# A transformer block on one core: in the attention loop the transposed scores go ahead of the scores for the maximum, an output half is copied out right behind its group, and the projection stage's normalization and loads are reordered

## The reference

```python
def _L0_attn_ref(x, Wq, bq, Wk, bk, Wv, bv, Wo, bo):
    Q, K, V = proj(Wq, bq), proj(Wk, bk), proj(Wv, bv)
    Q = Q * cos + _rotate_half(Q) * sin
    K = K * cos + _rotate_half(K) * sin
    scores = jnp.einsum('bhqd,bhkd->bhqk', Q, K) / scale
    scores = jnp.where(causal, scores, jnp.float32(-jnp.inf))
    attn = jax.nn.softmax(scores, axis=-1)
    out = jnp.einsum('bhqk,bhkd->bhqd', attn, V)
    return out.transpose(0, 2, 1, 3).reshape(B, S, H) @ Wo.T + bo
def _L0_ffn_ref(...):
    hdn = silu((xf @ gate_w.T) * gate_s) * ((xf @ up_w.T) * up_s)
    return (hdn @ down_w.T) * down_s
x = x + _L0_attn_ref(_layernorm(x), ...)
x = x + _L0_ffn_ref(_layernorm(x), ...)
```

## Time and profile before

| | |
|---|---|
| runs | 768.98, 772.01, 768.7 us |
| profiled execution | 772.27 us, its span 770.6 us |
| PE busy | 740.3 us (96%), 3563 instructions |
| PEld busy | 540.8 us (70%) |
| DVE busy | 437.1 us (57%) |
| ACT busy | 303.1 us (39%) |
| POOL busy | 245.6 us (32%) |
| chain that ended last | PE 75%, DVE 6%, ACT 5%, issue 5%, DMA 5% |
| TensorE's granted clock | 0.997 of full speed on the mean |

### The profile page before, as it was taken

One profiled execution on the slowest core, in us unless ns is written; L12 is line 12 of the kernel. 1 busy time (PEld: TensorE's weight loads), 2 busy tenths in 40 slices (PEclk: granted clock), 3 DMA queues, 4 the chain that ended last, 5 costly groups with the idle time before them and its releaser, 6 DMA issues.

```text
span 770.6 us, 10665 instructions
## 1 busy us (share of the span) xinstructions
PE 740.3 (96%) x3563; PEld 540.8 (70%) x3563; DVE 437.1 (57%) x1103; ACT 303.1 (39%) x641; POOL 245.6 (32%) x224
## 2 busy tenths in 40 slices
PE   7998999989999999999999989999999999999996
PEld 7786888765555555555555546787788888888885
DVE  7868493987777767777777726783325114315112
ACT  3231222255555555555555563223332223223221
POOL 0724161502114141414141416832223223223223
PEclk9999999999999999999999999999999999999999
DMA  8584659645656666666566554680001001001001
GB/s 279 210 280 166 219 202 298 257 134 153 155 157 184 157 174 157 166 155 182 157 181 157 141 158 136 223 353 0 1 1 55 0 1 54 0 0 56 0 1 57
DMA packets 54318, 104.39 MB, mean 135 GB/s; under 512 B 14820, under 2 KB 18404, under 8 KB 53748
## 3 DMA queue, kind: packets, MB, share of 16 engines
q1 hardware_dynamic: 54264, 103.72, 44.0%
HBM read 69.62 MB, written 38.21 MB: 140 GB/s over the span
## 4 chain that ended last, share of the span: by engine, by line
PE 75%; DVE 6%; ACT 5%; issue 5%; DMA 5%; POOL 2%; SPq 1%; DVEq 0%; POOLq 0%; ACTq 0%
PE ps L1096 31%; PE ps L1235 17%; PE ps L1311 9%; PE ps L1121 8%; PE ps L1214 8%; ACT p L679 4%; DMA x_st<-in_x 2%; PE ps L1088 1%; ACT o_raw L686 1%; DMA q_st<-neg_max_T 1%; POOL hid_lo L592 1%; DMA w_st<-in_wk 1%; DVE stats L770 1%; DVE xn L785 1%; DMA rec_l<-rec_rows 1%
## 5 line engine op out<-in xcount | busy, mean ns | idle before, releaser
L679 ACT ACTIVATE p<-ps 128x384 f32<-128x384 f32 (+3 forms) x384 | 162.5, 487 | 127.3 <-PE ps L1214 126.8
L842 DVE CUSTOM_DVE_ANT_0 masked<-ps,mask_qk 128x512 bf16<-128x512 f32 (+1 forms) x240 | 114.3, 502 | 77.3 <-PE ps L1121 76.2
L1235 PE MATMUL ps<-p,v_slot 128*64 128x512 f32 (+3 forms) x768 | 137.3, 493 | 7.7 <-ACT o_raw L686 7.6
L1214 PE MATMUL ps<-q_st,k_st 99*128 99x384 f32 (+2 forms) x384 | 134.8, 369 | 2.0 <-DMA q_st<-neg_max_T 1.1
L1121 PE MATMUL ps<-k_st,q_st 96*128 96x512 f32 (+2 forms) x384 | 130.8, 362 | 1.5 <-DVE row_max L842 1.3
L1047 DVE SCALAR_TENSOR_TENSOR hid<-ps,us_sb,silu 128x512 f32<-128x512 f32 x44 | 33.0, 750 | 165.2 <-PE ps L1096 159.5
L592 POOL TENSOR_TENSOR hid_lo<-hid,hid_hi 128x512 fp32r<-128x512 f32 x44 | 56.8, 1290 | 173.0 <-ACT hid_hi L757 173.0
L1235 PEld LDWEIGHTS ps<-p,v_slot 128*64 128x64 f32 x768 | 53.0, 136 | 80.8 <-issue 55.6
L561 POOL TENSOR_SCALAR_AFFINE_SELECT p<-p 128x512 f32<-128x512 f32 x64 | 41.0, 641 | 214.3 <-ACT p L679 214.3
L1121 PEld LDWEIGHTS ps<-k_st,q_st 96*128 96x128 f32 x384 | 72.2, 189 | 31.3 <-issue 21.8
L1214 PEld LDWEIGHTS ps<-q_st,k_st 99*128 99x128 f32 x384 | 72.2, 189 | 20.7 <-ACT p L679 8.8
(11 more groups left out here) (119 smaller groups left out, 1075.1 us busy)
## 6 DMA issues: line engine op xcount, KB each, us to landing
qk_scratch<-st_hi SPq DMA_DIRECT2D x32, 512.0 KB, 3.8
q_st<-qk_scratch SPq DMA_DIRECT2D x32, 384.0 KB, 4.1
k_st<-qk_scratch SPq DMA_DIRECT2D x32, 384.0 KB, 5.2
flag_st<-in_ffn SPq DMA_DIRECT2D x32, 264.0 KB, 2.8
ffn_copy<-in_ffn SPq DMA_DIRECT2D x32, 264.0 KB, 3.3
qk_scratch<-st_lo SPq DMA_DIRECT2D x16, 512.0 KB, 3.7
o_T<-o_raw SPq DMA_DIRECT2D x32, 128.0 KB, 4.1
rec_l<-rec_rows SPq DMA_DIRECT2D x32, 128.0 KB, 3.4
```

What stands on the lines that cost most here:

```text
L679: act.activation(p32[:, at:at + q0 + w - keep], ps[:, ST_BANK + i % ST_RING, keep - q0:w], ACT.Exp, scale=SCALE).then_inc(exp_done, 1)
L842: ins = dve.tensor_tensor_reduce((masked_a if u < 2 else masked)[:, s_before(i) % 2, col:col + kept], scores, mask_qk[:, 512 - kept:512], ...
L1214: pe.matmul(ps[:, ST_BANK + i % ST_RING, 0:w], k_st[0:K_ALL, slot, kt * P:(kt + 1) * P], q_st[0:K_ALL, slot, q0:q0 + w], start=True, stop= ...
L1235: ins = pe.matmul(ps[VW * a:VW * (a + 1), o_bank(u, half), q0 - 512 * half:512], v_slot[:, slot, kt, :], p32[:, at:at + n], start=(kt == 0 ...
```

## The change

Four orders change; no instruction is added or removed.

1. TensorE, stage B: at each position `shifted_piece(t, i)` is issued before `transpose_max(t + 1)` or `score_bank(t + 2, i)`, not behind it.
2. ScalarE, stage B: `evacuate_half(u, 0)` comes behind exponential 3 instead of exponential 6 of an even step.
3. VectorE and ScalarE, stage A: in chunks 1 and 2 the next chunk's statistics come before `rotate(0)` and its normalization directly behind it (before: behind `rotate(0)` and behind `low(0)`), and `std_of` ahead of `high(0)`. In chunk 0 the statistics come ahead of `weight_lo(3)`, and `std_of(1)` ahead of `weight_hi(5)`.
4. SyncE, stage A: the load of chunk `c + 2` of x is issued in chunk `c` ahead of the stores of `p` = 3, not at the start of chunk `c + 1`. For chunk 2 this takes it past those stores and past `load_late` (Wo's load).

```diff
@@ sync
             for c in range(N_CH):
                 b, cc = divmod(c, CC)
-                if 2 <= c + 1 < N_CH:
-                    sp.wait_ge(ln_done, c + 2)
-                    load_x(x_st[:, :, :], c + 1).then_inc(x_in, 16)
...
                 for p in range(4):
+                    if p == 3 and c + 2 < N_CH:
+                        sp.wait_ge(ln_done, c + 3)
+                        load_x(x_st[:, :, :], c + 2).then_inc(x_in, 16)
@@ scalar
                 if c == 0:
                     weight_hi(4)
+                elif c < N_CH - 1:
+                    std_of(c + 1)
                 high(0)
                 if c == 0:
+                    std_of(1)
                     weight_hi(5)
-                if c < N_CH - 1:
-                    std_of(c + 1)
                 high(1)
...
-                    if t % 2 == 0 and t >= 2 and i == PV_AFTER[0][0] + 3:
+                    if t % 2 == 0 and t >= 2 and i == PV_AFTER[0][0]:
                         evacuate_half((t - 2) // 2, 0)
@@ vector
+                def next_statistics():
+                    dve.wait_ge(x_in, 16 * (c + 1))
+                    ln_first(c + 1, x_tiles)
+                def next_tokens():
+                    dve.wait_ge(t_ps, TJ * (c + 1))
+                    ln_second(c + 1)
+                if 0 < c < N_CH - 1:
+                    next_statistics()
                 rotate(0)
                 if c == 0:
+                    next_statistics()
                     weight_lo(3)
-                if c == N_CH - 1:
+                elif c < N_CH - 1:
+                    next_tokens()
+                else:
                     dve.wait_ge(row_max_init, 1)
                     dve.wait_ge(ln_done, N_CH + 1)
-                if c < N_CH - 1:
-                    dve.wait_ge(x_in, 16 * (c + 1))
-                    ln_first(c + 1, x_tiles)
                 rotate(1)
                 low(0)
-                if 0 < c < N_CH - 1:
-                    dve.wait_ge(t_ps, TJ * (c + 1))
-                    ln_second(c + 1)
...
@@ tensor
                 for i in range(NPC):
+                    if t < HEADS:
+                        shifted_piece(t, i)
                     if i == M_ENTRY and t < HEADS - 1:
                         transpose_max(t + 1)
                     elif i != M_ENTRY and t + 2 < HEADS:
                         score_bank(t + 2, i)
-                    if t < HEADS:
-                        shifted_piece(t, i)
```

More of the change, by code:

```diff
@@ L925, in _ @@
                 if c == 0:
-                    dve.wait_ge(t_ps, TJ)
-                    ln_second(1)
+                    next_tokens()
                 if c == N_CH - 1:
```

## The result

| | before | changed |
|---|---|---|
| runs, us | 768.98, 772.01, 768.7, 771.51, 770.85 | 766.8, 763.55, 764.84, 762.3, 765.38 |
| median | 770.85 | 764.84 |
| profiled execution (span) | 772.27 (770.6) | 766.8 (765.1) |
| ratio | | 0.9924, 95% interval 0.99 to 0.9947 |

The change makes the kernel 6.0 us or 0.76% faster.

What follows compares the result with a forecast made beforehand. TensorE, busy 740.3 of 770.6 us, was taken as the bound, so only its waits or slow clock could be won. Terms 1.8 + 4.4 + 0.8 + 0.3 = 7.3 us gave 763.4 us, range 759 to 768.5.

Steps and rivals of the forecast that it cites:

- one of its signs: Projections, chunk 0: TensorE's p = 3 would run without a gap, where it stood idle 1.57 us before.
- Chunk 1, forecast 4.4 us: Projections, chunk 1: earlier x removes the stalls for rotate(1) and rotate(2) and the lower clock; 4.4 us, bounds 2 and 4.5.
- The second rival: Projections: x comes too late and, with statistics ahead of rotate(0), delays everything; 4.4 falls to 1 or 2, 766 us; chance 0.13.
- Chunk 0, forecast 1.8 us: Projections, chunk 0: statistics fill VectorE's 2.00 us wait, so TensorE's stall at p = 3 goes; 1.8 us, bounds 0 and 2.0.
- weight_lo(3) 1.7 more: Chunk 0, VectorE: after the statistics end at 22.8, weight_lo(3) takes 1.7 us and ends at 24.5, ahead of rotate(1).
- Attention, forecast 0.05 us in a pair: Attention, pair of steps: -0.12 ahead of group 0, +0.07 odd step, 0 even step; 0.8 us in 15 pairs.
- The 0.3 us from steps 0 and 1: Attention's first two steps: pieces run ahead of TensorE's wait for VectorE's maxima; 0.3 us gained.
- Attention gives it back: Rival: projections gain, but score banks behind waiting pieces cost 5.4 us against 6.2, leaving about 768 us; chance 0.17.
- Attention gains more: Rival: ScalarE's earlier start carries through, 13 us at most in 15 pairs; half gives about 757 us; chance 0.10.
- The slower case: Rival: each step's first piece waits for the maximum's rows, 0.5 us in each of 31 steps; 778 us; chance 0.05.
- The sum itself, 7.3 us: Whole kernel: 1.8 for chunk 0, 4.4 for chunk 1, 0.8 for attention pairs and 0.3 for steps 0 and 1.
- the middle between 765.0 and 761.7: Forecast median 763.4 us, between 7.3 off the profiled 772.27 and 7.3 off the median 768.98.

Runs made afterwards that it cites:

- e4: Kernel before with only the load of x for chunks 2 and 3 issued ahead of the stores of p = 3; ratio 0.9955.
- e5: Kernel before with only VectorE's and ScalarE's new order in the projections, x loaded at the old place; ratio 1.0107, slower.
- e6: Changed kernel, but at positions 5 to 9 the shifted piece again goes behind the score bank; ratio 0.9913 to the kernel before.
- e10: e7 with the DRAM-to-DRAM copy of feed-forward weights issued behind the next head's loads; ratio 0.9882 to the kernel before.
- e1: Kernel before with only the projection changes: VectorE's and ScalarE's new order and the early load of x; ratio 0.9948.
- e7: e6 with the copy of half 1 moved to directly behind its group, behind exponential 9 of the odd step; ratio 0.9858 to the kernel before.
- e8: Changed kernel with the copy of half 1 moved behind exponential 9 of the odd step; ratio 0.9916 to the kernel before.
- e2: Kernel before with only TensorE's attention order changed, shifted piece ahead of the score bank at each position; ratio 0.9993.
- e9: Kernel before with the early load of x and both output halves copied early, old orders elsewhere; ratio 0.9871.
- e11: e9 with the DRAM-to-DRAM copy of feed-forward weights issued behind the next head's loads; ratio 0.9862 to the kernel before.
- e12: e9 with VectorE's test of the feed-forward weights moved from behind position 3 to behind position 9; ratio 0.9986 to the kernel before.

## Why the prediction was right

The forecast was 763.4 us with a range of 759 to 768.5; the median is 764.84. The largest term was right in cause and size. One term was mis-sized, and one of its signs failed: chunk 0's p = 3 still has a gap of 0.88 us in the profile.

**Chunk 1, forecast 4.4 us: right.** It gave 4.49, the clock included. The late load was named as the cause, and e4 shows that it alone gives the whole term. What the prediction did not say is that part 3 gives nothing in this chunk; by e5 it needs the early load and costs 4.4 us without it. The second rival had this danger right and its size too small. It was near: rotate(1) ended 0.3 us before it was wanted, where 0.6 were forecast. The load was issued at 45.17 and not at about 42.3, and the chunk itself began at 48.74 and not at 46.1, so the margin shrank by only 0.3.

**Chunk 0, forecast 1.8 us: the term that was mis-sized.** In this pair of profiles, from p = 1 to V's first product (16.65 to 35.09 before, 18.17 to 35.93 now), it gave 0.68. The step that failed is "weight_lo(3) 1.7 more": it took 3.44. The rows show a wait in it: GpSimd's operation ran from 23.84 to 26.25, and VectorE's ended at 27.33, 1.08 us behind it, while the same operation takes 1.19 us where it meets nothing. Even the 1.77 us of before held such a wait (GpSimd until 22.65, VectorE until 23.74, 1.09 behind), and the prediction carried that number over.

The meeting is not in every execution. Seven executions with the old order in this chunk stalled for 1.57, 0, 1.39, 0, 1.42, 1.53 and 1.63 us, seven with the new one for 0.88, 0, 0, 0.86, 0, 0 and 0.87; on the mean 1.08 against 0.37. The three stalls of the new order are those of the changed kernel, e6 and e10, the three of these seven that had the lower clock from 10 to 12 us: in these VectorE reached weight_lo(3) 1.2 to 1.5 us later than in e1, just behind GpSimd's start (3.43 or 3.44 us). In the other four (e1, e5, e7, e8) it took 1.19 us and the stall was gone, as forecast. e1 and e6, both with VectorE's new order:

```profile
22.49 1.19 DVE L827 TENSOR_TENSOR w_lo<-w_st,w_hi 128x1024 fp32r<-128x1024 f32 x1
23.91 2.41 POOL L522 TENSOR_TENSOR w_lo<-w_st,w_hi 128x1024 fp32r<-128x1024 f32 x1 [1.43 <-ACT w_hi L620]
```

```profile
23.70 2.40 POOL L522 TENSOR_TENSOR w_lo<-w_st,w_hi 128x1024 fp32r<-128x1024 f32 x1
23.74 3.43 DVE L827 TENSOR_TENSOR w_lo<-w_st,w_hi 128x1024 fp32r<-128x1024 f32 x1
```

From p = 1 to V's first product those four took 16.34 to 16.78 us, and the five stalled executions of the old order 18.28 to 18.51. The two old executions without a stall, e2 and e4, took 16.93 and 16.34. So where the old order stalled and the new one did not meet GpSimd, the term was there, 1.5 us or more; elsewhere there was less to win or nothing. The prediction had no step for either.

**Attention, forecast 0.05 us in a pair: right, by its steps.** Ahead of group 0 0.19 instead of 0.12, the odd step's positions 4 to 9 +0.09 instead of +0.07, the even step's +0.03 instead of 0; the sum is as forecast. The rule that matmuls keep the program's order ("TensorE: Matmul & The Clock Gate" of the Trainium skill, Part 2, step 1) named the cost, and the trace agrees: the score bank at 245.13 started behind the piece that had waited until 244.91, though VectorE had emptied its bank at 244.74. The 0.3 us from steps 0 and 1 did not come: from chunk 3's start to the first group it took 55.28 us instead of 55.03. And what the prediction took for a small gain hides a cost: with both copies early, the pieces-first order loses 0.22 us in a pair (e8 against e9).

**The rivals.** "Attention gives it back" did not happen: e2 has 19.12 in a pair and a ratio of 0.9993, where it would have needed 19.5. "Attention gains more" did not happen either, but e7 and e9 show that moving ScalarE's copy takes the wait ahead of group 0 away: e9 wins 0.53 us there (5.39 to 4.86). The slower case had the right weak spot: the maximum's rows held TensorE up in single steps of most kernels, for 1.7 us here (1.1 before), and for 2.1 to 3.2 us in e7, e8 and e9, whose steps are shorter.

**The step from the profile to the median.** The prediction took the middle between 765.0 and 761.7, since the profiled 772.27 lay 3.3 above a median of three runs. With five runs the median before is 770.85, and beside the experiments it was 770.56 to 771.59. Three runs that spread over 3.3 us did not fix it. The middle amounts to 5.6 us off a median that was 1.9 too low, which lands near 764.84 partly by luck. The sum itself, 7.3 us, was 1.3 too large against the measured 6.0. In the two profiles chunk 0 came out 1.1 short and steps 0 and 1 another 0.55; how the unprofiled runs divide is not known.

## What to carry to other kernels

When an engine waits for one that works in order, read what stands ahead of the awaited instruction and what that waits for: here one late load was the whole stall of chunk 1, and reordering the work around it was worth nothing there and cost 1% of the kernel without the load. A copy that frees a buffer belongs directly behind the work that fills it, in the idle time of the engine that copies, before anything is reordered on the bound engine. Test such parts together as well as apart: the pieces-first order won 0.03 us in a pair alone and lost 0.22 beside both copies. Several waits taken off TensorE here were followed by another (VectorE's maxima, the two rows of 4 KB, an operation held up by GpSimd's), so a gain per step should be bounded by the next chain before it is multiplied by the steps.

## What the runs showed of the hardware

- VectorE's and GpSimd's operations on these SBUF tiles took turns where they met. weight_lo(3) started 0.04 or 0.05 us behind GpSimd's operation and took 3.43 or 3.44 us (changed kernel, e6, e10), ending 1.07 to 1.09 behind it; it takes 1.19 where it meets none (e1). In e5 VectorE's began first (23.57) and took 1.19, and GpSimd's (24.21) took 2.83 instead of 2.41. The weights' test in e11 took 2.44 instead of 0.70 and ended 0.57 behind GpSimd's scaling. In e11 one DMA issued later was enough to make the two meet.
- The granted clock from 10 to 12 us was 0.50 in the changed kernel's profile, with 1.95 us of waiting just before, and full in that of before, with 1.54. e11 waited 1.95 us there too and kept the full clock. Up to the second projection this costs 1.52 us (18.17 against 16.65, of which 0.10 were there before 10 us), and it differs between executions of the same code.
- The maximum's two rows of 4 KB each held TensorE up for 0.2 to 1.3 us at a time, in none to five steps of an execution (six, and up to 2.0 us, in e12); with one DMA of 264 KB out of their way, in none or one.
